# Eight layers on one core: the next pair's first feed-forward part and second attention are moved inside the expert part of the pair ahead, its first attention in front of that

## The reference

```python
x = x + LN(L0_attn(LN(x)))   # delta rule, chunks of 32, four heads
x = x + LN(L0_ffn(LN(x)))    # fp6 quantised linear layer
x = x + LN(L1_attn(LN(x)))   # RWKV: two scans over the tokens
x = x + LN(L1_ffn(LN(x)))    # two layers of local attention and a gated MLP
x = x + LN(L2_attn(LN(x)))   # 16 heads, causal
x = x + LN(L2_ffn(LN(x)))    # 16-head attention, then 2 of 8 experts
x = x + LN(L3_attn(LN(x)))   # linear attention
x = x + LN(L3_ffn(LN(x)))    # fp4 quantised gated MLP
```

```python
# L0_ffn: blocks of 32 features, scale = max|block| / 7.5, nearest value of the fp6 grid
out = dequant(quant(x)) @ dequant(quant(weight)).T + bias
# L1_attn: c is k, v, r
c = (x * mix_c + last_x * (1 - mix_c)) @ Wc.T        # last_x: x one token earlier
wkv_t = (alpha + exp(u + k_t) * v_t) / (beta + exp(u + k_t))
alpha, beta = ew * alpha + exp(k_t) * v_t, ew * beta + exp(k_t)
out = (wkv * sigmoid(r)) @ Wo.T
```

## Time and profile before

| | |
|---|---|
| median of 3 runs | 3885.82 us (3872.63 to 3893.88) |
| the profiled execution | 3877.94 us, its span 3876.2 us |
| granted TensorE clock, mean of the span | 0.86 |
| PE busy | 3013.8 us (78%) |
| DVE busy | 2396.4 us (62%) |
| ACT busy | 1523.8 us (39%) |
| POOL busy | 773.7 us (20%) |

### The profile page before, as it was taken

One profiled execution on the slowest core, in us unless ns is written; L12 is line 12 of the kernel. 1 busy time (PEld: TensorE's weight loads), 2 busy tenths in 40 slices (PEclk: granted clock), 3 DMA queues, 4 the chain that ended last, 5 costly groups with the idle time before them and its releaser, 6 DMA issues. The chain is left out here.

```text
span 3876.2 us, 90034 instructions
## 1 busy us (share of the span) xinstructions
PE 3013.8 (78%) x35930; PEld 2032.2 (52%) x35930; DVE 2396.4 (62%) x6722; ACT 1523.8 (39%) x3093; POOL 773.7 (20%) x823
## 2 busy tenths in 40 slices
PE   4667888997567788889755878888975577888896
PEld 2534565655444456565543445656544344565654
DVE  6675665557567466555767755754575675575457
ACT  4244534423414443442341544444234144444422
POOL 4131212101213221210121321121012132212101
PEclk8678999998668899999866889999986688999997
DMA  1011000000001100000000110000000011000000
GB/s 40 6 41 30 18 2 3 15 21 2 7 6 41 32 15 3 2 15 21 1 8 6 44 32 12 3 2 15 21 1 8 6 44 32 12 3 3 15 21 7
DMA packets 65274, 59.83 MB, mean 15 GB/s; under 512 B 16403, under 2 KB 54212, under 8 KB 64838
## 3 DMA queue, kind: packets, MB, share of 16 engines
q1 hardware_dynamic: 63606, 53.24, 5.1%
q10 hardware_dynamic: 1232, 0.61, 0.1%
HBM read 36.29 MB, written 2.10 MB: 10 GB/s over the span
## 5 line engine op out<-in xcount | busy, mean ns | idle before, releaser
L1321 POOL TENSOR_TENSOR l1t_ss<-l1t_ss,neghalf 128x16 f32<-128x16 f32 x64 | 243.1, 3798 | 452.2 <-DVE l1t_ss L1355 452.2
L167 POOL TENSOR_TENSOR ln_y_rstd<-ln_var_eps,neghalf 128x4 f32<-128x4 f32 x64 | 64.8, 1013 | 1004.6 <-DVE ln_var_eps L188 968.0
L2247 ACT ACTIVATE l2r_P<-l2r_bank_score 128x512 f32<-128x512 f32 x320 | 173.7, 595 | 178.2 <-PE l2r_bank_score L1969 178.2
L2247 ACT ACTIVATE l2a_P<-l2a_bank_score 128x512 f32<-128x512 f32 x320 | 173.7, 595 | 177.7 <-PE l2a_bank_score L1969 177.7
L1532 PE MATMUL l1t_ring<-l1f_qkv,x_normT 128*128 128x512 f32 x384 | 224.6, 716 | 18.9 <-DMA l1f_tables<-in_l_tables 10.2
L2139 DVE CUSTOM_DVE_ANT_0 l2a_masked<-l2a_bank_ring,l2a_neg_wide 128x512 bf16<-128x512 f32 (+1 forms) x256 | 148.9, 622 | 76.5 <-PE l2a_bank_ring L1938 75.2
L2139 DVE CUSTOM_DVE_ANT_0 l2r_masked<-l2r_bank_ring,l2r_neg_wide 128x512 bf16<-128x512 f32 (+1 forms) x256 | 148.7, 622 | 76.7 <-PE l2r_bank_ring L1938 76.4
L1969 PE MATMUL l2a_bank_score<-l2a_q_head,l2a_k_head 32*128 32x128 f32 x2560 | 190.5, 287 | 3.0 <-DMA l2a_q_head<-l2a_shiftT 1.6
L1938 PE MATMUL l2a_bank_ring<-l2a_k_head,l2a_q_head 32*128 32x128 f32 x2432 | 178.9, 288 | 16.0 <-DVE l2a_m L2139 7.1
L1938 PE MATMUL l2r_bank_ring<-l2r_k_head,l2r_q_head 32*128 32x128 f32 x2432 | 174.0, 284 | 19.9 <-DVE l2r_m L2139 9.9
L1969 PE MATMUL l2r_bank_score<-l2r_q_head,l2r_k_head 32*128 32x128 f32 x2560 | 186.2, 282 | 2.7 <-DMA l2r_q_head<-l2r_shiftT 1.2
(11 more groups left out here) (633 smaller groups left out, 7761.7 us busy)
## 6 DMA issues: line engine op xcount, KB each, us to landing
l1t_v_low<-l1t_v SPq DMA_DIRECT2D x112, 130.0 KB, 2.4
l2e_w<-in_L_ffn_w SPq DMA_DIRECT2D x96, 128.0 KB, 2.2
l1f_qkv<-in_L_ffn_wqkv SPq DMA_DIRECT2D x8, 768.0 KB, 4.3
l1f_tables<-in_l_tables SPq DMA_DIRECT2D x8, 512.0 KB, 5.7
l1f_w<-in_L_ffn_w SPq DMA_DIRECT2D x8, 341.0 KB
x_in<-in_L_attn_hidden_states SPq DMA_DIRECT2D x10, 256.0 KB, 3.0
l1f_wo<-in_L_ffn_wo SPq DMA_DIRECT2D x8, 256.0 KB, 4.7
l2a_q_head<-l2a_shiftT SPq DMA_DIRECT2D x128, 2.0 KB
```

The lines of the kernel that those rows point to most:

```text
L167: pool.tensor_tensor((b.yrs if post else b.rs)[:, p, :], b.ve[:, p, :], b.neghalf[:, 0:NT], ALU.pow).then_inc(s["post_rstd"] if post else ...
L1321: pool.tensor_tensor(ss[:, n % 2], ss[:, n % 2], b.neghalf[:, 0:2 * H8], ALU.pow).then_inc(s["rn_ready"], 1)
L2247: act.activation(self.P[:, use % self.P_RING].rearrange("k h q -> k (h q)"), self.score_bank(h, g)[:, :], ACT.Exp, scale=self.scale).then_ ...
```

## The change

The work is shifted by a part of a pair. In front of the loop the first pair's `l0_attn`, `l0_ffn` and `l1_attn` run alone. The loop has three turns; a turn begins with `l1_ffn` of a pair, and between its second attention and its `l2_ffn` the next pair's `l0_attn` runs (alone on the engines, as before). The next pair's `l0_ffn` and `l1_attn` have no blocks of their own in the loop: their instructions are laid between those of the experts, in the new `l2_ffn_experts_and_front`. Behind the loop the last pair runs from `l1_ffn` to the end, with the old expert code. The next pair's residual stays in `x_in` for this.

In the new function VectorE's extra work is a generator, `front()`, cut into 67 steps by `yield`; `advance` takes steps in the places that the table `SIDE` gives (between the two halves, behind the second half, behind the addition). TensorE's and ScalarE's extra work has fixed places by unit. Both use one pair of banks, `turned`, for transposes and products.

Two more things change. The mixing of `l1_attn` is folded into the weights: with `now = mix * W` and `W - now` worked out once in `prepare`, each of k, v and r is two products summed in a bank, and VectorE's four mixing steps per sequence are gone. And in both expert functions the gate's second part (`choose`) comes behind the first `hid` products instead of ahead of all of them. `next_x` moves to the start of the third attention (`l2_attn`).

```diff
-        with nc.Fori(0, NIT) as it:
...
-            for (_, run), w in zip(layers, weights):
-                before = run(nc, b, w, before)
...
+        before = l0_attn(nc, front, w0a, [])
+        before = l0_ffn(nc, front, w0f, before)
+        before = l1_attn(nc, front, w1a, before)
+        store(before, None)
+
+        with nc.Fori(0, NIT - 1) as it:
...
+            before = l1_ffn(nc, b, front, w1f, [])
+            before = l2_attn(nc, b, w2a, before)
+            before = l0_attn(nc, front, w0a, before)
+            before = l2_ffn_attention(nc, b, w2f, before)
+            before = l2_ffn_experts_and_front(nc, b, front, w2f, w0f, w1a, before)
+            before = l3_attn(nc, b, w3a, before)
+            before = l3_ffn(nc, b, w3f, before)
+            store(before, out_pairs[it])
...
+        before = l1_ffn(nc, b, front, w1f, [])
+        before = l2_attn(nc, b, w2a, before)
+        before = l2_ffn_attention(nc, b, w2f, before)
+        before = l2_ffn_experts(nc, b, w2f, before)
+        before = l3_attn(nc, b, w3a, before)
+        before = l3_ffn(nc, b, w3f, before)
...
+SIDE = [(0, 0, 0), (1, 1, 3), (1, 1, 3), (1, 1, 3), (1, 1, 3), (1, 1, 3), (1, 1, 2), (1, 1, 1), (1, 1, 2),
+        (0, 1, 1), (1, 1, 1), (1, 1, 3), (1, 1, 2), (1, 1, 1), (1, 1, 2), (1, 1, 2)]
...
+            def front():
...
+                yield from pre_stats(s0, step0, 0)
+                yield from pre_stats(s0, step0, 1)
+                negative_mean(s0, 0)
+                negative_mean(s0, 1)
+                yield
+                yield from quantise(0)
+                yield from quantise(1)
+                yield from post_rows(s0, step0, 0)
+                yield from add_rows(s0, step0, 0)
...
+                yield from pre_stats(s1, step1, 0)
+                negative_mean(s1, 0)
+                yield
+                yield from post_rows(s0, step0, 1)
+                yield from add_rows(s0, step0, 1)
...
+                yield from pre_stats(s1, step1, 1)
+                negative_mean(s1, 1)
+                yield
+                yield from denominator(0)
+                yield from numerator(0)
+                yield from denominator(1)
+                yield from numerator(1)
...
+                yield from post_rows(s1, step1, 0)
+                yield from add_rows(s1, step1, 0)
+                yield from post_rows(s1, step1, 1)
+                yield from add_rows(s1, step1, 1)
...
+            advance(1)
+            compare(0)
+            multiply(0, 0)
+            choose(0)
+            multiply(0, 1)
+            compare(1)
+            choose(1)
+            for n in range(1, len(experts)):
+                multiply(n, 0)
+                advance(SIDE[n][0])
+                multiply(n, 1)
+                advance(SIDE[n][1])
+                add(n - 1)
+                advance(SIDE[n][2])
+            add(len(experts) - 1)
+            for _ in side:
+                pass
...
+            def exp_k(p):
+                warm(act, b, ACT.Exp, 4 * p + 2)
+                act.wait_ge(s1["k_ready"], p + 1)
+                act.activation(ek[:, p, :], turned[p][:, :], ACT.Exp).then_inc(s1["exp_k_ready"], 1)
+                act.activation(euk[:, p, :], turned[p][:, :], ACT.Exp,
+                               bias=w_att["u"][:, 0:1]).then_inc(s1["exp_uk_ready"], 1)
+                warm(act, b, ACT.Silu, 4 * p + 3)
...
+            for n in range(len(experts)):
+                up(n, 0)
+                if n == 4:
+                    turn(s0, s0["xq_ready"], xq, 0)
+                if n == 6:
+                    turn(s0, s0["xq_ready"], xq, 1)
+                if n == 8:
+                    turn(s1, s1["xn_act"], f.xn, 0)
+                if n == 10:
+                    project("v", 0, s1["exp_r_ready"], s1["v_ready"])
+                    turn(s1, s1["xn_act"], f.xn, 1)
+                if n == 12:
+                    result(0)
+                if n == 15:
+                    result(1)
+                up(n, 1)
+                if n == 4:
+                    feed_forward(0)
+                if n == 6:
+                    feed_forward(1)
+                if n == 8:
+                    project("k", 0, s1["xT_ready"], s1["k_ready"])
+                if n == 9:
+                    project("r", 0, s1["exp_uk_ready"], s1["r_ready"])
+                if n == 10:
+                    project("k", 1, s1["xT_ready"], s1["k_ready"])
+                if n == 11:
+                    project("r", 1, s1["exp_uk_ready"], s1["r_ready"])
+                if n == 12:
+                    project("v", 1, s1["exp_r_ready"], s1["v_ready"])
+                if n:
+                    down(n - 1)
...
@@ def l1_attn(nc, b, w, before):
+                for c, ps, ready in (("k", k_ps, s["k_ready"]), ("v", v_ps, s["v_ready"]), ("r", r_ps, s["r_ready"])):
+                    pe.matmul(ps[p][:, :], w["now_" + c][:], b.xT[:, p, :], start=True, stop=False)
+                    pe.matmul(ps[p][:, :], w["w" + c][:], b.xT_pad[:, p, 3:3 + S], start=False, stop=True).then_inc(ready, 1)
```

More of the change, by code:

```diff
@@ L160, with pow_rstd @@
 QUANT_SHARE = (2, 4)
-def pow_rstd(pool, b, s, post=False, first=False):
+def pow_rstd(pool, b, s, post=False, first=False, behind=None):
     for p in range(PAIR):
@@ L174, in pow_rstd @@
         if not first:
-            own(pool.tensor_tensor(b.offset[:], b.offset[:], b.gain[:], ALU.add))
+            own(pool.tensor_tensor(b.offset[:], (behind or b).offset[:], b.gain[:], ALU.add))
             own.settle()
@@ L1695, in _ @@
             if last_layer:
[L1696 removed]
+                pow_rstd(pool, b, s, post=True, behind=f)
         @block.vector
@@ L1773, in _ @@
                 last.then_inc(s["y_ready"], 1)
-        return s.values()
+        return [*s.values(), b.x_stored] if last_layer else s.values()
 H16 = 16
```

580 lines of the change are left out of this document (476 added, 104 removed).

## The result

The changed kernel took 3720.27 us (median of 4 runs, 3710.13 to 3733.83) against 3879.23 before: a ratio of 0.9589, 95% interval 0.9543 to 0.9635. That is 4.1% faster. Forecast were 3732, with 3695 to 3785 as the range. On another chip the same pair gave 0.9606 (0.9584 to 0.9629). The profiled execution took 3722.94 us, its span is 3721.2.

The account below looks back on a forecast made before the run. TensorE was taken to bound the experts, and only their own order the two moved parts. The span 3876.2 - 222.9 + 90 - 6 - 5 - 3 = 3729.3 us gave a forecast time of 3732, range 3695 to 3785.

Parts of the forecast that it names:

- Removed: Loop: the first feed-forward part and second attention vanish as blocks in three turns, 3 x 74.3 = 222.9 us less.
- Added to the experts: Expert stage: interleaved VectorE and TensorE work adds 30 us per stage, 90 in all; bounds 20 and 45 per stage.
- The head: Start of the expert stage: four steps before the router wait add 1.6 us, a single gate wait gives back 0.4.
- In a unit the longer engine decides: Expert units 1 to 15: the longer of VectorE and TensorE sets each, sum 102.6 us, 24.3 more than 78.3.
- The bias pairs: TensorE in the experts: bias products cost 2.9 us per sequence, halved with the clock; bounds 1.8 and 5.8.
- the waits add up: Rival, 24 in 100: waits on the shared banks hold up the experts, 40 to 45 us per stage, 3761 to 3776.
- The tail: End of the expert stage: one addition of 1.2 us stands alone.
- the signs that were named in advance: Profile after: expert stage 134 us, clock 0.90 or more, units 4, 6, 10 longest, bias pairs 0.36, one border less.
- The first attention, moved: Following a stage at clock 0.96 saves 3 us each of three; next attention 1 more each; net -6 us.
- Borders: Loop returns: three become two, -5 us, between -7 and 0.
- Once only: Outside the loop: first pair's mixing steps about 3 us less, last pair's earlier `hid` about 1.7; net -3.
- the rival with the lower clock: Rival, 4 in 100: TensorE falls to the lower clock in the experts, 119 us more per stage, time 3998.

Follow-up runs that it names:

- apart: Changed kernel with the next pair's first feed-forward part and second attention as blocks of their own in the loop, no overlap: 3843.79 us, 0.991 of before.
- experiment 7: Changed kernel with nine quantiser steps on VectorE working on 8 columns instead of 512, rounding left out: 3716.48 us, single run.
- experiment 6: Changed kernel without the bias and with only one of the two products for each of k, v and r on TensorE: 3690.63 us, single run.
- experiment 12: Changed kernel with one 128-row bias product per sequence, late first output product and VectorE's side steps two earlier: 3694.53 us, 0.9509 of before.
- the filler: Ten small TensorE products at the first attention's head, added to the changed kernel with one 128-row bias product and late output product: 3708.64 us.
- bias_none: Changed kernel with the bias left out of the interleaved function: 3727.35 us, single run.

## Why the prediction was right, and where it was not

**Removed: right.** The loop has no such blocks, and the forecast of 225.9 with the first pair's share came out at 224.7.

**Added to the experts: right in size, 83 us for three stages against 90 (398.0 for 315.0), but not by its parts.** The forecast per stage was +1.2 at the head, 23.4 in units 1 to 14 (96.5 for 73.1), 2.1 in the last unit and the tail, and 3 for handovers. Measured in the first turn: -4.5 in the head and unit 0, +26.9 in units 1 to 14, +5.3 in the last unit and tail.

- *The head* was mis-sized with the wrong sign. The new gate order had no term in the loop's sum; the 0.4 there is for a single wait. The four steps ahead of the router cost nothing visible, and TensorE no longer waits for a `hid` that stands behind the whole gate (from its first `up` on, unit 0 is 4.0 us for 8.2). In `apart`, with nothing beside the experts, head and unit 0 take 11.6 for 16.5, so it is the gate order, and with it the clock: before, three of the four stages had it at its lower level over most of the first `up` of unit 0, and in the changed kernel's loop none had.
- *"In a unit the longer engine decides"* failed for VectorE's units. I gave units 1, 2, 3, 5, 13 and 14 35.6 us; they took 33.0. Unit 1, 1.1 over, has the same 6.5 in `apart`, so that the other five took 3.7 less than I gave them. VectorE may lag behind for several units, since TensorE only waits for its `hid`, and it makes up for it later (experiment 7: without 7.5 us of VectorE's work unit 3 loses 0.3 and units 2 and 5 nothing). The price was also too high: 52 us forecast, 102.73 - 57.25 = 45.5 measured. Part of that is the order: in its old place each step of the quantiser waits for the one ahead, and beside the experts a `hid` often stands between:

```profile
1820.00 0.69 DVE L2882 TENSOR_TENSOR l2x_q<-l2x_q 128x512 f32<-128x512 f32 x1
1820.72 0.69 DVE L2885 SCALAR_TENSOR_TENSOR l2x_q<-l2x_q 128x512 f32<-128x512 f32 x1
...
1822.66 0.68 DVE L2891 SCALAR_TENSOR_TENSOR l2x_q<-l2x_q 128x512 f32<-128x512 f32 x1
1823.26 0.68 DVE L3031 TENSOR_TENSOR l2x_hid<-l2x_silu,l2x_up 128x512 f32<-128x512 f32 x1
```

Dependent steps start 0.72 us apart, a step and an independent `hid` 0.60. The rule holds for TensorE in units 7 to 11, where it has no hole to catch up in (experiment 6).
- *The bias pairs* were taken at 0.36 us; they are 0.42 (3.3 per sequence for 2.9). The reason given, that everything halves with the clock, was wrong: 0.2 of it is the change of the operand's rows. What I had not seen at all is the clock behind them, 1.6 us in about every other such unit; in the profiled execution it stood in unit 4 of each turn.
- *The waits* of TensorE (1.55 in unit 6, 1.85 in unit 12, 1.7 in unit 15) are the rival "the waits add up" in small: 3 us were set aside for handovers, and units 6 and 12 have 3.4. The wait in unit 15 belongs to the tail.
- *The tail* was taken as one addition. VectorE is nearly full from unit 13 on (4.7 of 5.2 us, 5.1 of 5.3) and enters the tail late: 3 us more (experiment 12).

The errors nearly cancel: 29.7 forecast, 27.7 measured. That is luck: -5.7 in the head against +3.5 in the units and +3.2 in the tail, with 3 set aside. Of the signs that were named in advance, the stage (131.6 to 134.8), its clock and the single border came true. Unit 12 stands among the longest in place of unit 10, VectorE's units are near 5.3 and not 6, and the bias pair is at 0.42 for 0.36.

**The first attention, moved: the number was met, the reason fell.** Forecast -9 and +3, measured -5.8 and +1.8 in the profiled execution. I had said that the clock at entry saves 3 us, since the stage follows one at 0.96. (That TensorE begins at the upper level in the first pair is not in the rows named for it, but the trace has 1.00 over its first 20 us.) But the mean of the stage ahead says nothing of its end. Its last 6 us are at 0.54, and the first 10 of the moved one at 0.60; before, these first 10 were at 0.50 to 0.63 behind the border (second turn of the changed kernel, then of the kernel before):

```profile
1546.55:1552.55 6.00, 1.13 (x3) 0.64 (x3) 3.77 (x18) 0.32 (x2) 1.44 (x4) 0.54 0.00 1
1552.55:1562.55 10.00, 5.03 (x14) 2.80 (x15) 4.99 (x25) 5.61 (x11) 5.07 (x4) 0.60 0.01 2
```

```profile
987.14:997.14 10.00, 5.63 (x13) 2.80 (x14) 4.17 (x25) 5.37 (x10) 2.12 (x2) 0.50 0.02 5
```

The same code took between 112.5 and 120.4 us in the profiled executions of this kernel and of eleven of the experiments (without the filler), and the 36 cases inside their loops average 116.2, against 116.4 over the four of before (117.1 over the three behind a border, 113.4 to 119.0). The move is worth nothing that can be told from this spread, and nothing sets the -5.8 apart from chance. These two sets of windows, of this kernel and of `bias_none`, show the same stage from 30 us behind its start on: 47.5 us, 18 us and the rest:

```profile
1582.50:1630.00 47.50, 23.34 (x502) 21.80 (x491) 34.29 (x77) 22.09 (x70) 10.70 (x10) 0.50 0.01 2
1630.00:1648.00 18.00, 15.84 (x194) 14.70 (x190) 12.09 (x41) 3.45 (x6) 2.17 (x3) 0.94 0.00 1
1648.00:1667.30 19.30, 10.88 (x51) 9.83 (x50) 11.51 (x55) 1.38 (x2) 8.10 (x9) 0.62 0.00 1
```

```profile
1584.60:1632.10 47.50, 22.96 (x517) 21.30 (x518) 33.20 (x75) 23.23 (x76) 12.95 (x10) 0.51 0.01 2
1632.10:1650.10 18.00, 16.55 (x192) 15.58 (x190) 10.48 (x29) 3.45 (x6) 1.98 (x2) 0.78 0.00 1
1650.10:1675.00 24.90, 15.86 (x70) 14.47 (x69) 14.32 (x68) 1.40 (x3) 8.29 (x9) 0.57 0.00 1
```

Up to 88 us from the start the same instructions stand within about 1 us of each other. But from 78 us on the clock stays up in the one (0.94 over 18 us) and falls early in the other (0.78), and the stage ends 5.6 us later. All 56 first attentions of the fourteen profiled executions fall into three groups by the clock of these 18 us, the part behind VectorE's triangular solve: at 0.93 to 0.97 the stage takes 112.5 to 114.8 us (20 cases), at 0.84 to 0.88 it takes 115.9 to 117.3 (16), at 0.75 to 0.78 it takes 118.0 to 120.4 (20). The entry doesn't decide it: the first pair's stage starts at 1.00 in all but the one with the filler, and takes anything from 112.9 to 120.2.

**Borders: right.** -5 forecast, -4.9 measured: the fourth feed-forward part with its border is 58.1 in the last turn and 61.8 to 62.1 in the two others. **Once only: right** within 1 us, by two errors: its gate term was 2.8 instead of 1.7, and the mixing ahead of the first scan 1.6 (72.7 for 74.3) instead of 3.

**Third attention: forecast 0, measured -4.9, and it is the clock again.** In all four turns before, the granted clock falls for 3.4 us about 58 us into the stage, and what follows stands 1.3 us later; in the changed kernel it doesn't fall there in any. In the other kernels with this code the stage takes 132.6 to 135.0 us, and once 144.6.

**The rivals.** The mean clock of the expert stage is 0.92 to 0.94, and the lower level comes for some 3 us at a time and at the tail. So the rival with the lower clock did not come. The Trainium skill ("TensorE: Matmul & The Clock Gate", A second HAM failure mode: psum-queue depth-cycling) expects swings from short idles between groups. The trace agrees in part: unit 12's wait of 1.85 us was followed by slow products in 7 of the 24 stages that have it and in none of the 12 in which `up` fills it. But the more frequent fall here came behind one-row products with TensorE busy throughout. ScalarE's table loads cost 1.28 us and no draining in the new stage too:

```profile
1870.92 0.58 ACT L3087 ACTIVATE l2x_exp_r<-l2x_turned 128x512 f32<-128x512 f32 x1
...
1871.52 1.28 ACT L256 ACT_TABLE_LOAD   x1
...
1872.92 0.58 ACT L3094 ACTIVATE l2x_silu<-l2x_up 128x512 f32<-128x512 f32 x1
```

The load begins 0.60 us after the exponential did, right at its end, and the SiLU 0.12 us behind the load. By the Trainium skill's extra 1.38 us ("ScalarE: Activation LUTs", What ACT_TABLE_LOAD costs) there would be a hole on one side of the load; the trace does not agree.

## What to carry to other kernels

Work of another stage can fit beside a stage that is bound by one engine at the price of its own instructions on that engine. It did to within a tenth of a microsecond in units 7 to 11, where that engine waits for nothing; so price its queue first, and let the others lag, as long as they have caught up where it waits for them. Then look in that queue for waits that have ready work behind them, and put the ready work ahead: one such move and a bias without one-row products gave 0.5% on one chip, and with the lagging engine's steps two places earlier it was 0.7 to 0.8% (against medians from other chips). And when a stage's time in the profile changes by a few us with unchanged code, ask how the same stage varies between executions before giving it a reason.
